# A perceiver block: waits by block, another PSUM bank, three row tiles as split products, wide constant products, one tile moved

## The reference

```python
x = x + cross_attention(layernorm(x), ctx)      # 16 heads of 32; Wq, Wk, Wv, Wo with biases
x = x + linear_attention(layernorm(x))          # elu(.)+1 features, 128 per head; w_qkv, proj, w_out, b_out
x = x + moe(layernorm(x))                       # router, 16 experts, shared expert
# moe: scores = softmax(h @ gate_w.T) over experts; each expert takes its best 8 of the 64 rows
# of every batch (64 slots); eo = (gelu(x_tok @ Wg.T) * (x_tok @ Wu.T)) @ Wd.T * weight, scattered
# back by addition; the shared expert (1024 hidden units) is applied to all rows
```

## Time and profile before

| | us |
|---|---|
| median of 3 timed runs | 662.16 |
| their range | 661.93 to 662.62 |
| profiled execution, its own time | 661.46 |
| its span | 659.7 |

### The profile page before, as it was taken

How to read it: one execution, slowest core, us unless ns; L and a number is a source line. 1 busy time by engine, 2 the same in 40 slices (tenths; PEclk the granted TensorE clock), 3 DMA queues, 4 the chain that set the end, 5 groups by cost and what they waited for, 6 DMA issues and landing times.

```text
span 659.7 us, 10426 instructions
## 1 busy us (share of the span) xinstructions
PE 642.0 (97%) x4232; PEld 417.4 (63%) x4232; DVE 311.3 (47%) x643; ACT 254.4 (39%) x488; POOL 33.4 (5%) x38
## 2 busy tenths in 40 slices
PE   8999999999999999999999988999999999999997
PEld 7867777777878786678878665444443444443433
DVE  4864735445453615754778785323313232323123
ACT  5554635454544535546685252212121212111210
POOL 0000300000000001535000000000000000000000
PEclk9999999999999999999999999999999999999999
DMA  8211010110340000030229635989999999999972
GB/s 290 109 65 65 1 66 8 57 63 3 126 194 1 1 1 2 1 112 19 113 72 433 241 149 203 377 362 387 405 417 411 401 404 397 391 377 392 364 298 77
DMA packets 14348, 129.56 MB, mean 196 GB/s; under 512 B 2720, under 2 KB 2848, under 8 KB 6240
## 3 DMA queue, kind: packets, MB, share of 16 engines
q1 hardware_dynamic: 12576, 127.15, 49.5%
q10 hardware_dynamic: 1728, 1.77, 0.8%
HBM read 125.90 MB, written 1.05 MB: 192 GB/s over the span
## 4 chain that ended last, share of the span: by engine, by line
PE 82%; DVE 5%; ACT 5%; DMA 4%; ACTq 2%; issue 1%; SPq 0%; DVEq 0%
PE ps L1225 24%; PE ps L1511 14%; PE ps L1548 7%; PE ps L1521 5%; PE ps L1418 5%; DMA w_u<-in_wu 4%; PE ps L1296 4%; PE ps L1367 3%; PE ps L1561 3%; PE ps L1272 3%; PE ps L1235 2%; PE ps L1307 2%; PE ps L1465 2%; PE ps L1338 2%; ACTq L397 2%; PE ps L1477 1%
## 5 line engine op out<-in xcount | busy, mean ns | idle before, releaser
L1548 PE MATMUL ps<-w_d,hid_T 128*64 128x512 f32 x256 | 58.2, 596 | 1.4 <-ACT hid_T L772 1.4
L1511 PE MATMUL ps<-w_u,x_slot 128*64 128x512 f32 x256 | 58.1, 595 | 0.9 <-DMA w_u<-in_wu 0.9
L1511 PE MATMUL ps<-w_g,x_slot 128*64 128x512 f32 x256 | 58.1, 595 | 0.8 <-ACT x_slot L788 0.8
L584 ACT ACTIVATE probs<-ps,neg_max 128x512 f32<-128x512 f32 x64 | 43.5, 688 | 38.9 <-DVE neg_max L907 38.9
L750 ACT ACTIVATE hid<-ps 128x512 f32<-128x512 f32 x24 | 14.4, 598 | 102.5 <-PE ps L1511 76.8
L1225 PE MATMUL ps<-wv_hi,ctx_hi 128*128 128x512 f32 x128 | 51.5, 402 | 0.0
L887 DVE COPY probs_T<-ps 128x512 f32<-128x512 f32 x28 | 19.4, 692 | 64.9 <-PE ps L1296 64.9
L1225 PE MATMUL ps<-wv_lo,ctx_hi 128*128 128x512 f32 x128 | 50.0, 390 | 0.0
L1225 PE MATMUL ps<-wv_hi,ctx_lo 128*128 128x512 f32 x128 | 49.8, 389 | 0.0
L907 DVE TENSOR_REDUCE neg_max<-ps 128x1 f32<-128x512 f32 x64 | 39.7, 683 | 18.2 <-PE ps L1272 18.2
L1085 DVE TENSOR_TENSOR hid<-hid,ps 128x512 f32<-128x512 f32 x24 | 16.5, 687 | 65.4 <-PE ps L1511 35.9
(11 more groups left out here) (249 smaller groups left out, 1175.8 us busy)
## 6 DMA issues: line engine op xcount, KB each, us to landing
w_u<-in_wu SPq DMA_DIRECT2D x16, 2048.0 KB, 15.7
w_d<-in_wd SPq DMA_DIRECT2D x16, 2048.0 KB, 11.8
w_g<-in_wg SPq DMA_DIRECT2D x16, 2048.0 KB, 13.1
ctx_raw<-in_ctx SPq DMA_DIRECT2D x7, 1024.0 KB, 4.8
w_qkv<-in_wqkv SPq DMA_DIRECT2D x1, 3072.0 KB, 15.0
ws_g<-in_wsg SPq DMA_DIRECT2D x1, 2048.0 KB, 9.1
ws_u<-in_wsu SPq DMA_DIRECT2D x1, 2048.0 KB, 7.8
ws_d<-in_wsd SPq DMA_DIRECT2D x1, 2048.0 KB, 21.9
```

Of the source, the lines that this page charges most:

```text
L584: act.activation(probs[:, p, :], bank(SCORE[p]), ACT.Exp, bias=neg_max[:, p:p + 1], scale=1.0, accum_out=row_sum[:, p:p + 1]).then_inc(exp ...
L1511: ins = pe.matmul(ps[64 * fh:64 * (fh + 1), dst, :], x_slot[:, e, dt, :], weights[e % 2][:, dt, BANK * fh:BANK * (fh + 1)], start=(dt == 0 ...
L1548: ins = pe.matmul(ps[64 * fh:64 * (fh + 1), 6 + side(n), :], hid_T[:, side(n), j, 64 * fh:64 * (fh + 1)], w_d[e % 2][:, KT * fh + j, :], s ...
```

## The change

Seven edits:

1. WARM goes from 16 products of 128 columns to 9 of 512 columns (the same `ones`, broadcast four times).
2. The first three row tiles of the cross residual become split products. POOL makes the parts of `o_T` batch by batch for batches 0 to 5, and after batch 6's values the parts of `w_o`. They lie in tiles that are free by then (`xn_hi`, `xn_lo_cross`, `ctx_hi[:, 0]`, `ctx_lo[:, 0]`). The fourth row tile stays plain. All of this stands on POOL between `add_row_bias` and the fill of `v_bd`.
3. The gate product of item 1 waits block by block for its slot copies.
4. The last routing matrix is transposed into bank 5 and read from there.
5. The wait for all of `give_done` moves: 4 before `item_down(2)`, 5 before `item_transpose(3)`.
6. `item_up` gets a hook `each(dt)` for edit 3.
7. At the end the down tile 3 of the last stripe moves behind `item_transpose(LAST)`.

```diff
+        o_hi, o_lo, w_o_hi, w_o_lo = xn_hi, xn_lo_cross, ctx_hi[:, 0], ctx_lo[:, 0]
...
+        SPLIT_ROWS = B - 2
-        WARM = 16
+        WARM = 9
...   (POOL, behind add_row_bias(0, bo_rows))
+            for b in range(SPLIT_ROWS):
+                cols = slice(L * b, L * (b + 1))
+                pool.wait_ge(o_done, b + 1)
+                pool.tensor_copy(o_hi[:, :, cols], o_T[:, :, cols]).then_inc(o_hi_done, 1)
+                pool.wait_ge(o_hi_done, b + 1)
+                pool.tensor_tensor(o_lo[:, :, cols], o_T[:, :, cols], o_hi[:, :, cols].bitcast(F32),
+                                   ALU.subtract).then_inc(o_split, 1)
+            pool.wait_ge(wo_in, 16)
+            pool.wait_ge(v_ps, (B - 1) * NS)
+            for dt in range(KT):
+                pool.tensor_copy(w_o_hi[:, dt], w_o[:, dt]).then_inc(wo_hi_done, 1)
+            for dt in range(KT):
+                pool.wait_ge(wo_hi_done, dt + 1)
+                pool.tensor_tensor(w_o_lo[:, dt], w_o[:, dt], w_o_hi[:, dt].bitcast(F32), ALU.subtract).then_inc(wo_split, 1)
...   (DVE)
-            dve.tensor_scalar(give_last[:].rearrange("p t c -> p (t c)"), bank(4), last_weight[:, E - 1:E], None,
+            dve.tensor_scalar(give_last[:].rearrange("p t c -> p (t c)"), bank(5), last_weight[:, E - 1:E], None,
...   (TensorE)
-                pe.matmul(ps[:, LN_BANK, 0:P], ones[:], ones[:], start=True, stop=True)
+                pe.matmul(bank(LN_BANK), ones[:], ones[:].unsqueeze(1).to_broadcast([P, KT, P]), start=True, stop=True)
...
             def cross_residual(t):
-                pe.wait_ge(o_done, 2 * (t + 1))
-                residual(0, t, o_T, w_o)
+                if 2 * (t + 1) > SPLIT_ROWS:
+                    pe.wait_ge(o_done, 2 * (t + 1))
+                    residual(0, t, o_T, w_o)
+                    return
+                pe.wait_ge(o_split, 2 * (t + 1))
+                toks = slice(P * t, P * (t + 1))
+                product3(bank(RES_BANK[0][t]), (lambda dt: o_hi[:, dt, toks], lambda dt: o_lo[:, dt, toks]),
+                         (lambda dt: w_o_hi[:, dt, :], lambda dt: w_o_lo[:, dt, :])).then_inc(res_ps, 1)
             pe.wait_ge(wo_in, 16)
+            pe.wait_ge(wo_split, KT)
...
-            pe.wait_ge(slot_done[0], 2 * KT - len(BY_DVE))
-            pe.wait_ge(slot_done[1], len(BY_DVE))
-            item_gate(1)
+            def copied(dt):
+                g = KT + dt
+                by_dve = sum(d <= g for d in BY_DVE)
+                pe.wait_ge(slot_done[0], g + 1 - by_dve)
+                if by_dve:
+                    pe.wait_ge(slot_done[1], by_dve)
+            item_up(1, w_g, None, 0, wg_in, g_ps, copied)
...
-                ins = pe.transpose(ps[:, 4, P * t:P * (t + 1)], give_last_T[:, t].rearrange("p h s -> p (h s)"), ident[:])
+                ins = pe.transpose(ps[:, 5, P * t:P * (t + 1)], give_last_T[:, t].rearrange("p h s -> p (h s)"), ident[:])
             ins.then_inc(give_ps, 1)
-            pe.wait_ge(give_done, 5)
             for n in range(3, LAST - 1):
                 if n > 3:
                     item_gate(n)
+                if n == 4:
+                    pe.wait_ge(give_done, 5)
                 item_transpose(n - 1)
                 item_value(n)
+                if n == 3:
+                    pe.wait_ge(give_done, 4)
                 item_down(n - 1)
...
-            item_down(LAST_SHARED, (2, 3))
+            item_down(LAST_SHARED, (2,))
             item_transpose(LAST)
+            item_down(LAST_SHARED, (3,))
```

More of the change, by code:

```diff
@@ L296, in perceiver_block @@
         attT_ps, attT_done = sem("attT_ps"), sem("attT_done")
+        wo_hi_done, wo_split, o_hi_done, o_split = sem("wo_hi_done"), sem("wo_split"), sem("o_hi_done"), sem("o_split")
         logit_ps, lsub_done, lexp_done, score_done = (
@@ L1498, in _, with item_up @@
             moe_transpose(2)
-            def item_up(n, weights, shared_parts, off, in_, done):
+            def item_up(n, weights, shared_parts, off, in_, done, each=None):
                 dst = 2 * (side(n)) + off
@@ L1509, in item_up @@
                     for dt in range(KT):
+                        if each:
+                            each(dt)
                         for fh in range(2):
```

## The result

| | before | after |
|---|---|---|
| median of the timed runs | 661.94 (661.02 to 662.62) | 657.53 (656.75 to 659.22, 6 runs) |
| profiled execution, its own time | 661.46 | 657.60 |
| its span | 659.7 | 655.7 |

The ratio is 0.9939, with an interval from 0.9929 to 0.9949: faster by 4.0 us. The prediction was 4.1 us and a time of 658.1; the median is 657.53. The profiled execution gained 3.9 of its own time. So the total is right. The terms are less so: two were too small, and a loss that no term held took 1.4 back.

What follows compares the result with a forecast made beforehand. TensorE, busy for 97% of the 659.7 us span, was taken as the bound. Terms 1.6 + 0.1 + 0.9 + 1.0 + 0.5 = 4.1 took 661.46 to 657.4, or 658.1 against the timed runs; range 655.6 to 660.2.

Steps and rivals of the forecast that it cites:

- WARM: Start: wide constant products raise TensorE's clock 4.1 us sooner; gain 1.6 us, bounds -0.1 and 1.6.
- rival B: Start: the clock doesn't rise earlier, so the 1.6 is gone; 2.5 left, 659.7; chance 0.13.
- The cap: Start: ACT's second v_s copy, ending at 25.51, frees the fourth value tile's bank and limits the gain to 1.6.
- Split tiles: End of cross attention: TensorE saves 2.05, but DVE's chain collides with POOL; gain 0.1, bounds -0.2 and 2.05.
- the branch in which tile 0's normalise waits: End of cross attention: it waits for POOL's first subtraction, ends at 269.3; tile 1's normalise then ends at 273.8.
- Rival A: End of cross attention: milder POOL collision, the split tiles' 2.05 arrives whole; 6.1 gained, 656.0; chance 0.2.
- Slot waits: First expert: its gate follows the gather at once instead of waiting for DVE's last slot copy; gain 0.9.
- bank: Expert stage: with bank 5, the transposes behind the last routing matrix no longer wait for DVE; gain 1.0.
- tail tile: End: with down tile 3 moved behind them, the last hid transposes start earlier; gain 0.5, bounds 0 and 0.55.
- Rival C: Expert stage: the loads swallow its 1.9, the stream's pace being set before 458; 2.2 left, 660.0; chance 0.1.
- Rival E: Near 275: TensorE's 2 us hole lets the clock fall, costing 2.5 to 4; about 661.5; chance 0.05.
- Rival D: Cross attention batches: POOL's o_T splits hold DVE up; six batches lose 7.8, time 665.9; chance 0.04.

Runs made afterwards that it cites:

- before with wide products and fill: Kernel before with 9 wide constant products at the start and six more into bank 5 ahead of the routing products: 659.28, ratio 0.9973.
- the hold: Changed kernel with POOL waiting for DVE's normalise of row tile 2 before its first weight split: 655.57, ratio 0.9909.
- the hold with the fill: Changed kernel with POOL held until DVE's normalise of tile 2, and six wide constant products ahead of the routing products: 654.54, ratio 0.9901.
- the filled one: Changed kernel with six unread constant products of 512 columns ahead of the routing products: 656.65, ratio 0.9938.
- the fill: Six unread wide constant products into bank 5 ahead of the routing products, tried in four kernels; alone in the kernel before: 660.73, ratio 0.9991.

## Why the prediction was right, and where its terms were not

**WARM, predicted 1.6, passed on 2.14 in the profiles; worth 1.3 on the mean of the profiles and 1.2 in the cleanest timed pair.** The pace did rise earlier, in all six profiles with wide products (rival B falls). The cap was the right mechanism, and 1.6 nearly its size, but "follows DVE's statistics of x, which nothing here moves" was read as a fixed time, and it is not one: no edit moves it, but Wv's load does. By the rule above the wide products in before's execution, with Wv at 13.91, would have reached 24.92 + 5.3 = 30.2, a gain of 1.45; before with wide products and fill, its Wv at 13.88, came at 30.20. The rest up to 2.14 is Wv's early landing in the changed kernel's execution. Also, 10.7 was the latest rise of all narrow starts (project_v 17.54 to 19.01 in six kernels, 16.70 to 17.09 with wide products). "One rise in one trace is all I have" stood in the text, and the term took it nonetheless. The Trainium skill (TensorE: Matmul & The Clock Gate, "What's actually happening") says that one and the same kernel sees its clock rise at different times; the table agrees, for the six kernels whose start is the same.

**Split tiles, predicted 0.1, measured 0.53.** The steps held: POOL ready in time, tile 1's chain in POOL's run, the wait on probs_T, a hole near 275. POOL's copy was 0.57, not 1.0, in full cover. The step that was off is the branch in which tile 0's normalise waits, "from 269.3 I get 273.8". POOL's run is over at 272.64 by the prediction's own reading, so in neither branch could tile 1's normalise be held to 273.1; from 272.64 with the plain 0.55 it ends at 273.2. The runs show just that. With before's first tile as the zero (2.11 added) the normalise ended at 269.0 and tile 1's product began at 271.7. By then only POOL's last subtraction was left, so one wait followed, to 272.7, and not a second one on the normalise. The add came at 273.2 instead of 273.8, against 273.72 before. Rival A (2.05 arrives whole) fell for this change, and is what the hold brings: 1.98. The Trainium skill's lock on the shared port pair (SBUF — State Buffer, "SBUF: two separate sides") fits the 1.01 that ends exactly with POOL's instruction, and the adds that read one operand from PSUM, 0.68 beside POOL, 0.68 or 0.69 without it.

**Slot waits 0.9, bank 1.0, tail tile 0.5:** measured 0.91, 1.0 and 0.52. These three were read off waits in the trace whose end the edit names, and each passed on whole. No run has the tail tile by itself, but from the last w_u to the last w_d it is 5.89 or 5.90 in the five profiles with it and 6.40 to 6.43 in the eight without.

**Loads.** Rival C falls: the lead grew from 3.08 to 3.42 in the expert stage, and the hold with the fill, 6.25 ahead on the last w_u, waits no longer there than before. The wait for the last w_u scatters from 0 to 1.15 between profiles; the 0.3 by which it was shorter in the changed kernel lies within that scatter, and so does the 0.56 by which it was longer in the filled one.

**Not in the sum: the clock at the gather, 1.45 lost in the profiled execution.** Rival E had a fall of the clock, at the wrong hole. Through the 1.15 idle near 275 the granted clock stayed at 1.00 (windows 272 to 277); it fell in the router's thin stretch, where no wait of TensorE is over 1.29. It is not something that the change brought in, since the kernel before has it in 40 of 73 runs; its profile just did not show it, and the changed kernel's did. Whether the change makes it more frequent (4 of 6) no run tells. So the two surpluses (WARM 0.5, split 0.4), the 0.3 shorter wait for w_u and this loss made up 3.9 where 4.1 stood: the total was hit in part by luck, between two single executions that each could have had another start and another clock.

**Rival D** (o_T splits hold DVE up): nothing of it; the first row tile comes 2.11 earlier, as the first query product did (2.14), and with the split tiles alone 0.50 earlier, where its query product was 0.54 earlier.

**Open.** Why the clock falls in some executions and not in others of the same kernel; whether wide products make it more likely (without the fill it fell in 16 of 22 runs with them and in 64 of 124 with narrow ones; the gap is too small to tell); and where the wide products' runs up to 664.4 lost more than the 1.4 that the gather explains (the kernel before has one at 664.47 too). The fill removed both, which ties the scatter to the fall but does not show its path. Also open is why the wait for the last w_u scatters.

## What to carry to other kernels

A stall read off the trace with the edit at its end was worth its whole length in all three cases here. A stall that another engine's chain covers (DVE's norm beside POOL) must be asked how many of the other's instructions are left when the chain gets there, for each branch. When TensorE's part of a stretch is shortened, look at which engine pair collides there: a collision that cost nothing becomes the bound, and one wait that moves the other engine's work by 8 us gives the gain back.

A start time in one trace that hangs on a load or on the clock is a sample, not a constant. Before comparing two profiles, compare their clock rows at the thin stretches and the landing of the first loads; a difference of 2 us out of 660 can be these alone.

Where TensorE waits for a chain of small steps ahead of a dense stretch, a few constant products in the wait can keep the clock up: six of them, 1.5 us long, did here in 32 of 32 runs. The next product came 1.70 behind the last one ahead of them, against 1.68 and 1.67 without. What it gave in time was 0.1 to 1.0 us, so it has to be read from the profile.

## What the hardware showed that I had not expected

The start ran at the slow pace (fours 1.7 apart) while the granted clock's column read 1.00 for that very stretch in the kernel before; only at the gather did the column show 0.50:

```profile
5.40:10.60 5.20, 5.19 (x12) 4.12 (x13) 2.71 (x6) 2.52 (x5) 0.00 (x0) 1.00 0.96 273
```

So for the start of this kernel I read the clock from the distances between products, which is an inference: no row shows the low level there. It is not the loads that set the slow pace: in the changed kernel the fours are 0.9 apart with the DMA engines at a share of 1.06 (6.5 to 10), where before they were 1.7 apart at 0.96.

GpSimd copies fp32 to fp32r at 0.57 us for 128x512 (2.29 for four) and subtracts at 1.24 to 1.31 (4.97 to 5.22 for four).
